# A fused transformer block: shared-expert products moved among the last expert tiles, gathers re-paced, eight scatters held

## The chip, the cores and the metric

One core of a Trainium2 chip runs the whole program. The metric is the device time of one execution in microseconds; lower is better.

## What is computed

The input x has 4 batches of 512 tokens of 256 values. The block is feed-forward, attention, feed-forward, each with a residual:

```python
x = x + 0.5 * ffn(layernorm(x))
x = x + attention(layernorm(x))          # 16 heads of 128, weights as codes times scales
x = x + 0.5 * ffn(layernorm(x))
# ffn(h):
probs = softmax(h @ router_w.T)                              # 16 experts
topk_w, topk_idx = top_k(probs, 2); topk_w /= sum(topk_w)
shared = (silu(h @ shared_gate_w) * (h @ shared_up_w)) @ shared_down_w     # width 256
routed = for each token, sum over its 2 experts e of
         topk_w * (silu(h @ gate_w[e]) * (h @ up_w[e])) @ down_w[e]        # width 128
ffn = shared + routed
```

## The kernel before, in words

Each engine has a program of its own, written out by hand in one order, and semaphores tie the programs together; nothing else sets the order. f = 0 is the first feed-forward, f = 1 the second. The change touches f = 1 alone.

Values are kept as a high and a low part, and a product is three passes of TensorE (`product`, L1703 to L1705): high by high, high by low, low by high. So each result is first copied by ScalarE (the high part) and then subtracted by VectorE (the low part).

**Routing.** Batch by batch, rows of X are normalized, transposed (L1714), copied by ScalarE (`xt_hi`, L850) and split by VectorE (`xt_lo`, L1171); TensorE makes the router's logits (L1729 to L1732), VectorE chooses two experts for each token (`choose`; its last step, `marked`, L1210, raises `hot1`), and ranks and counts give each token its place. GpSimd scatters the normalized rows to `xs_dram`, in order of experts: four scatters of 128 rows for each of two choices, eight to a batch (`to_experts`, L597; for the first two batches `place`, L738). One more transfer (L793) fills the space behind each expert's rows. Scatters of batches 0 to 2 raise `scat0`, those of batch 3 `scat_3`. In the meantime SP loads the expert weights, 16 transfers of 768 KB.

**Expert tiles.** A tile is 128 rows of one expert; 48 tiles are worked in 24 pairs. SP loads the tiles (`tile_loads`, L494): it waits for the table `toff1`, for all of `scat0`, and ahead of pair 4 for `scat_3` and the fill. For pair p, TensorE transposes the rows of pair p + 1 (L1809), makes the gate and up products of pair p, transposes h of pair p - 1 (L1834) and makes the down product of pair p - 2. ScalarE copies rows (L876), applies SiLU (L888), copies h (L893) and evicts the result (L899, raises `r_ev`); VectorE splits (L1358, L1382) and multiplies (L1370). SP stores each pair's result to `y_tiles` (L465).

**Shared expert.** A step is one batch, in two products k (`gate_up(f, k)`, step k // 2): 12 multiplications of 512 columns each: a gate bank and an up bank, and for each two row blocks of the input in three passes. ScalarE applies SiLU (`shared`, L863), VectorE multiplies (`shared_mul`, L1338), ScalarE copies and VectorE splits (`shared_hi`, L868; `shared_lo`, L1343), TensorE makes the down product of the step (`down`, 24 multiplications of 256 columns), and VectorE adds it to X (`shared_add`, L1350). Products 0 to 3 come ahead of the tiles, `down(1, 1)` behind the first pair, products 4 to 7 and two down products behind the last pair.

**Combining.** GpSimd gathers each token's two rows from `y_tiles` (`fetch`, L605), eight gathers to a batch, and VectorE adds each, times its weight, to X (`combine_block`, L1395). Batch 0 is combined beside pairs 21 to 23, the others behind the pairs. `stored` waits until the tiles that a batch needs are in `y_tiles`; the counts for that are loaded into registers from `need`. Gathers are paced by `r_ev`: those of batch 0 one to a pair from pair 9 on. SP writes each half batch of X out when it is done.

## Time and profile before

| | us |
|---|---|
| median of 3 runs (1068.46 to 1069.44) | 1068.58 |
| the profiled execution, its own time | 1071.48 |
| its span | 1069.7 |
| TensorE busy | 980.6 (92% of the span) |
| VectorE busy | 798.7 (75%) |
| ScalarE busy | 676.3 (63%) |
| GpSimd busy | 626.3 (59%) |

The granted clock of TensorE over the span is 0.964 of full speed. The page gives shares over the whole program; a change in one stage is read from the rows of that stage. In the order of time, a row has its start, its duration, engine, line and operation, what is written and read, and in brackets how long the engine was idle before it and what released it. "issue" means that the profile shows nothing that it waited for, "remote" that the release came from something that the profile doesn't pair with an instruction. A line can be that of a helper, so that L1703 to L1705 stand for all three-pass products.

### The profile page before, as it was taken

Reading aid. Unit: us, or ns where it says so; the run is one execution under the profiler, and the core shown is the slowest. Engines: PE = TensorE matmul, PEld = TensorE weight load, DVE = VectorE, ACT = ScalarE, POOL = GpSimd, SP = SyncE. Lnnn points to the kernel's source line nnn. Section 1 sums busy time; section 2 is a strip of 40 time slices with the busy share of each in tenths; the row PEclk is TensorE's granted clock in tenths of the full one; section 3 lists DMA queues with packets and bytes.
Section 4 is the critical chain, followed back from the end, with each engine's and each line's share of the span. In section 5 each row is a group of like instructions: output and inputs, shape, how many; then the busy total and the mean of one; then the engine's idle time right before and its main releaser. Section 6 shows DMA issues by size and latency. Waiting matters only on the chain. (4 is left out here: it accounts for less than half of the span.)

```text
span 1069.7 us, 18752 instructions
## 1 busy us (share of the span) xinstructions
PE 980.6 (92%) x5314; PEld 844.7 (79%) x5314; DVE 798.7 (75%) x1682; ACT 676.3 (63%) x1485; POOL 626.3 (59%) x916
## 2 busy tenths in 40 slices
PE   5669999899999999999999999999999997579995
PEld 4459987677888888888888888888888885469985
DVE  7777577788887777787777877778788876358545
ACT  5545645667776777777776777767777765135641
POOL 1740458776436876767787666787536377630252
PEclk9769999999999999999999999999999999879997
DMA  9877652766456675787768877777754469966653
GB/s 313 286 254 236 199 188 69 152 152 115 79 100 142 138 128 105 188 182 182 150 142 210 216 190 159 172 149 185 162 97 80 87 146 197 391 234 197 194 177 104
DMA packets 329891, 183.07 MB, mean 171 GB/s; under 512 B 273344, under 2 KB 314944, under 8 KB 329152
## 3 DMA queue, kind: packets, MB, share of 16 engines
q1 hardware_dynamic: 323056, 155.66, 59.8%
q0 software_dynamic: 6432, 20.98, 5.9%
q10 hardware_dynamic: 304, 5.24, 1.4%
q8 instruction: 46, 0.75, 0.3%
q14 instruction: 53, 0.43, 0.1%
HBM read 73.31 MB, written 46.92 MB: 112 GB/s over the span
## 5 line engine op out<-in xcount | busy, mean ns | idle before, releaser
L669 POOL CAST R<-turned 128x512 fp32r<-128x512 f16 x512 | 290.5, 617 | 215.2 <-DMA turned<-work 152.4
L1703 PE MATMUL bank<-R 128*128 128x512 f32 (+2 forms) x1056 | 391.7, 371 | 25.3 <-DVE R L1343 10.0
L1704 PE MATMUL bank<-R 128*128 128x512 f32 (+2 forms) x1056 | 380.7, 360 | 0.0
L1705 PE MATMUL bank<-R 128*128 128x512 f32 (+2 forms) x1056 | 379.7, 360 | 0.0
L1703 PEld LDWEIGHTS bank<-R 128*128 128x128 f32 x1056 | 206.0, 195 | 59.5 <-issue 13.8
L1705 PEld LDWEIGHTS bank<-R 128*128 128x128 f32 x1056 | 205.7, 195 | 28.3
L1704 PEld LDWEIGHTS bank<-R 128*128 128x128 f32 x1056 | 206.2, 195 | 26.7
L975 ACT ACTIVATE bank<-bank,soft 128x512 f32<-128x512 f32 x256 | 170.3, 667 | 70.6 <-DVE soft L1515 70.6
L1508 DVE SCALAR_TENSOR_TENSOR R<-bank,bias,R 128x512 fp32r<-128x512 f32 x192 | 143.7, 749 | 68.5 <-ACT R L995 37.5
L1515 DVE TENSOR_REDUCE soft<-bank 128x1 f32<-128x512 f32 x256 | 168.6, 686 | 25.1 <-PE bank L1705 25.1
L1529 DVE SCALAR_TENSOR_TENSOR work<-bank,soft,work 128x512 f16<-128x512 f32 x256 | 185.1, 742 | 0.8 <-ACT work L988 0.8
L988 ACT ACTIVATE work<-bank,soft 128x512 f16<-128x512 f32 x256 | 161.5, 683 | 14.4 <-DVE soft L1523 14.1
L605 POOL DMA_INDIRECT R<-y_tiles,gpos x48 | 46.5, 969 | 124.7 <-ACT work L899 66.3
L1940 PE MATMUL bank<-R 128*128 128x512 f32 x256 | 104.6, 409 | 9.0 <-POOL R L669 7.3
L1941 PE MATMUL bank<-R 128*128 128x512 f32 x256 | 102.3, 400 | 0.0
L1942 PE MATMUL bank<-R 128*128 128x512 f32 x256 | 101.5, 396 | 0.0
L995 ACT ACTIVATE R<-bank,bias 128x512 fp32r<-128x512 f32 x64 | 44.1, 689 | 82.0 <-PE bank L1942 82.0
L969 ACT ACTIVATE R<-bank,bias 128x512 fp32r<-128x512 f32 x128 | 87.1, 681 | 0.0
L597 POOL DMA_INDIRECT xs_dram<-work,pos x48 | 50.6, 1053 | 48.4 <-DVE pos L1219 34.6
L1957 PE MATMUL bank<-R 128*128 128x256 f32 x256 | 72.3, 282 | 3.4 <-DVE R L1508 3.4
L1959 PE MATMUL bank<-R 128*128 128x256 f32 x256 | 72.4, 283 | 0.0
L1958 PE MATMUL bank<-R 128*128 128x256 f32 x256 | 72.4, 283 | 0.0
(164 smaller groups left out, 1379.2 us busy)
## 6 DMA issues: line engine op xcount, KB each, us to landing
work<-in_parts SPq DMA_DIRECT2D x64, 256.0 KB, 4.1
work<-in_ffn_w SPq DMA_DIRECT2D x34, 384.0 KB, 4.8
work<-xs_dram SPq DMA_DIRECT2D x96, 128.0 KB
y_tiles<-work SPq DMA_DIRECT2D x48, 256.0 KB
w_dram<-work SPq DMA_DIRECT2D x16, 768.0 KB, 4.6
R<-w_dram SPq DMA_DIRECT2D x16, 768.0 KB
y_tiles<-in_empty ACTq DMA_DIRECT2D x2, 2176.0 KB
X<-in_x SPq DMA_DIRECT2D x4, 512.0 KB, 4.9
```

Source lines behind the costliest of these rows:

```text
L669: nc.gpsimd.tensor_copy(whole_into(m, l, kb), whole_block(m, u, l, kb)).then_inc(s["cast_pool"], 1)
L975: nc.scalar.activation(s_bank(m, qb)[:], s_bank(m, qb)[:], ACT.Exp, bias=m.mx[:, qb:qb + 1], scale=1.0, accum_out=m.sm[:, qb:qb + 1]).then ...
L988: nc.scalar.activation(m.planes[:, qb, 0, :], s_bank(m, qb)[:], ACT.Copy, scale=m.ri[:, qb:qb + 1])\
L1508: v_.scalar_tensor_tensor(out=dst[:, 1, :], in0=bank[bk][:], scalar=m.bias[:, which, h:h + 1], in1=dst[:, 0, :].bitcast(F32), op0=ALU.add, ...
L1515: v_.reduce_max(m.mx[:, qb:qb + 1], s_bank(m, qb)[:], AX_X, negate=True).then_inc(s["max"], 1)
L1529: v_.scalar_tensor_tensor(out=m.planes[:, qb, 1, :], in0=s_bank(m, qb)[:], scalar=m.ri[:, qb:qb + 1], in1=m.planes[:, qb, 0, :], op0=ALU.m ...
L1703: nc.tensor.matmul(out, ah, bh, start=(i == 0 and first), stop=False)
L1704: nc.tensor.matmul(out, ah, bl, start=False, stop=False)
L1705: last = nc.tensor.matmul(out, al, bh, start=False, stop=(i == n - 1))
L1940: nc.tensor.matmul(bank[1][:], vh, ph, start=(kb == 0), stop=False)
L1941: nc.tensor.matmul(bank[1][:], vh, pl, start=False, stop=False)
L1942: ins = nc.tensor.matmul(bank[1][:], vl, ph, start=False, stop=(kb == QB - 1))
```

## The change

Six things, all in f = 1.

1. Shared products 4 and 5 are made inside the pair loop: product 4 at the pair index 23, product 5 at 24, each ahead of a pair's down product; ScalarE's and VectorE's steps of them go along. Products 6 and 7 follow the loop, ahead of both down products.
2. Own buffers: products 4 to 7 have banks 2 and 3 as gate banks (in place of 4 and 5), step 3 takes banks 0 and 1 for up and 4 and 5 for its down product, and step 2's h goes to `hT2`. Step 3's down product no longer waits for step 2's sums; the copy of its h waits for the last pair's down product instead.
3. The sums of step 3 come ahead of the second half of batch 3's combining, not behind all of it.
4. Gathers: two to a pair for each batch, from pairs 9, 16 and 20; before, one to a pair for batch 0 from pair 9, and two to a pair from 17 and 21. Batch 3's gathers wait for its stores and for product 5 alone, not for one of the products 4 to 7 each. The twelve counts are loaded at once.
5. Batch 3's gathers land in the part of xT that holds the tokens of batch 2, not in the experts' weights.
6. The eight scatters of the third batch wait for `hot1` = 4, the choice of the fourth batch.

```diff
 def shared_banks(f, step):
+    if (f, step) == (1, 3):
+        return 0, 4
     return (6, 0) if f == 0 and step < EARLY[0] else (0, 6)
+
+def gate_bank(m, f, k):
+    late = f == 1 and k >= 2 * EARLY[1]
+    return m.bank[(2 if late else 4) + k % 2]

 def turned_h(m, f, step):
-    return m.hT2 if (f, step) == (1, 1) else m.hT
+    return m.hT2 if (f, step) in ((1, 1), (1, 2)) else m.hT

-LANDING = {(0, 0): 0, (0, 2): 2, (0, 3): 3, (1, 0): 0, (1, 1): 1}
+LANDING = {(0, 0): 0, (0, 2): 2, (0, 3): 3, (1, 0): 0, (1, 1): 1, (1, 3): 2}
...
@@ pool_program
     pool.wait_ge(s["pos1"], 1)
+    pool.wait_ge(s["hot1"], QB)
     to_experts(1, 2, 0)
     to_experts(1, 2, 1)
...
-    stored(1, 0)
-    pool.wait_ge(s["gu"], 2 * QB + 2)
-    for j in range(TOPK * QB):
-        pool.wait_ge(s["r_ev"], NPAIR + SLOW_FROM + j)
-        fetch(1, 0, j)
-    stored(1, 1)
+    pool.wait_ge(s["need"], 2)
+    _, counts = nc.values_load_multi_w_load_instructions(
+        m.need[0:1, 0:RESULTS * B], engines=[POOL_ENGINE], min_val=16, max_val=2 * PUT_F)
+
+    def gathers(b, first):
+        for sem, n in zip(m.put, counts[RESULTS * b:RESULTS * (b + 1)]):
+            pool.wait_ge(sem, n)
+            pool.sem_inc(s["there"], 1)
+        pool.wait_ge(s["gpos"], TOPK * B + TOPK * (b + 1))
+        for j in range(TOPK * QB):
+            if first is not None:
+                pool.wait_ge(s["r_ev"], NPAIR + first + j // 2)
+            fetch(1, b, j)
+
     pool.wait_ge(s["gu"], 2 * QB + 4)
-    for j in range(TOPK * QB):
-        pool.wait_ge(s["r_ev"], NPAIR + SLOW_FROM + 8 + j // 2)
-        fetch(1, 1, j)
-    stored(1, 2)
+    gathers(0, SLOW_FROM)
+    gathers(1, SLOW_FROM + 7)
     pool.wait_ge(s["r_xt"], NPAIR + MOST)
-    for j in range(TOPK * QB):
-        pool.wait_ge(s["r_ev"], NPAIR + SLOW_FROM + 12 + j // 2)
-        fetch(1, 2, j)
-    stored(1, 3)
-    pool.wait_ge(s["r_dn"], 2 * NPAIR)
-    for j in range(TOPK * QB):
-        pool.wait_ge(s["gu"], 3 * QB + 1 + j // 2)
-        fetch(1, 3, j)
+    gathers(2, SLOW_FROM + 11)
+    pool.wait_ge(s["gu"], 2 * QB + 6)
+    gathers(3, None)
@@ act_program, shared_hi
-        wait(act, s["dn"], 2 * QB * f + 2 * (k // 2))
+        if (f, k // 2) == (1, 3):
+            act.wait_ge(s["r_dn"], 2 * NPAIR)
+        else:
+            wait(act, s["dn"], 2 * QB * f + 2 * (k // 2))
@@ act_program, tiles, ahead of the eviction
+            if f == 1 and p == NPAIR - 1:
+                shared(1, 4)
+            if f == 1 and p == NPAIR:
+                shared_hi(1, 4)
+                shared(1, 5)
@@ act_program, behind tiles(1)
-    for k in range(2 * EARLY[1], 2 * QB):
-        shared(1, k)
-        shared_hi(1, k)
+    shared_hi(1, 5)
+    shared(1, 6)
+    shared(1, 7)
+    shared_hi(1, 6)
+    shared_hi(1, 7)
@@ dve_program, tiles, at the end of a pair
+            if f == 1 and p == NPAIR - 1:
+                shared_mul(1, 4)
+            if f == 1 and p == NPAIR:
+                shared_mul(1, 5)
+                shared_lo(1, 4)
@@ dve_program, behind tiles(1)
-    shared_h(1, 4)
+    shared_lo(1, 5)
     combine_half(1, 1, 0)
-    shared_h(1, 5)
     combine_half(1, 1, 1)
-    shared_h(1, 6)
+    shared_mul(1, 6)
+    shared_mul(1, 7)
     shared_add(1, 2)
+    shared_lo(1, 6)
+    shared_lo(1, 7)
     combine_half(1, 2, 0)
-    shared_h(1, 7)
     combine_half(1, 2, 1)
     combine_half(1, 3, 0)
-    combine_half(1, 3, 1)
-    dve.wait_ge(s["comb1"], 2 * B)
     st.settle()
     shared_add(1, 3)
+    combine_half(1, 3, 1)
@@ pe_program, down
-            wait(pe, s["x_add"], 2 * QB * f + 2 * (step - 1) + i + 1)
+            if (f, step) != (1, 3):
+                wait(pe, s["x_add"], 2 * QB * f + 2 * (step - 1) + i + 1)
@@ pe_program, tiles, ahead of the down product of pair p - 2
+            if f == 1 and p in (NPAIR - 1, NPAIR):
+                gate_up(1, 4 + p - NPAIR + 1)
@@ pe_program, behind tiles(1)
-    gate_up(1, 4)
-    gate_up(1, 5)
+    gate_up(1, 6)
+    gate_up(1, 7)
     pe.wait_ge(s["r_ev"], 2 * NPAIR)
-    gate_up(1, 6)
     down(1, 2)
-    gate_up(1, 7)
     down(1, 3)
```

**ScalarE, the last two pairs and what follows.** L867 of the change is L863 of before (SiLU of a shared product), L875 is L868 (the copy of h), L895, L900 and L911 are L888, L893 and L899 (SiLU, copy and eviction of a pair). Before:

```order
L888 ACTIVATE work<-bank 128x256
L893 ACTIVATE R<-bank 128x256
L899 ACTIVATE work<-bank 128x512
L893 ACTIVATE R<-bank 128x256
L899 ACTIVATE work<-bank 128x512 x2
L863 ACTIVATE work<-bank 128x512
L868 ACTIVATE R<-work 128x512
L863 ACTIVATE work<-bank 128x512
L868 ACTIVATE R<-work 128x512
```

and now:

```order
L895 ACTIVATE work<-bank 128x256
L900 ACTIVATE R<-bank 128x256
L867 ACTIVATE work<-bank 128x512
L911 ACTIVATE work<-bank 128x512
L900 ACTIVATE R<-bank 128x256
L875 ACTIVATE R<-work 128x512
L867 ACTIVATE work<-bank 128x512
L911 ACTIVATE work<-bank 128x512 x2
L875 ACTIVATE R<-work 128x512
L867 ACTIVATE work<-bank 128x512 x2
L875 ACTIVATE R<-work 128x512 x2
```

The SiLUs of products 4 and 5 stand ahead of the evictions of pairs 21 and 22; those of 6 and 7 follow each other.

**VectorE, the end of its program.** L1352 is L1338 of before (multiply), L1357 is L1343 (split), L1364 is L1350 (sums), L1416 is L1395 (combining; eight rows of it are a batch). Before:

```order
L1338 TENSOR_TENSOR work<-bank,work 128x512
L1343 TENSOR_TENSOR R<-work,R 128x512
L1395 SCALAR_TENSOR_TENSOR X<-R,wt,X 128x256 x4
L1338 TENSOR_TENSOR work<-bank,work 128x512
L1343 TENSOR_TENSOR R<-work,R 128x512
L1350 SCALAR_TENSOR_TENSOR X<-bank,X 128x512 x2
L1395 SCALAR_TENSOR_TENSOR X<-work,wt,X 128x256 x4
L1338 TENSOR_TENSOR work<-bank,work 128x512
L1343 TENSOR_TENSOR R<-work,R 128x512
L1395 SCALAR_TENSOR_TENSOR X<-work,wt,X 128x256 x4
L1395 SCALAR_TENSOR_TENSOR X<-R,wt,X 128x256 x8
L1350 SCALAR_TENSOR_TENSOR X<-bank,X 128x512 x2
```

and now:

```order
L1352 TENSOR_TENSOR work<-bank,work 128x512
L1396 TENSOR_TENSOR R<-bank,R 128x256
L1352 TENSOR_TENSOR work<-bank,work 128x512
L1357 TENSOR_TENSOR R<-work,R 128x512 x2
L1416 SCALAR_TENSOR_TENSOR X<-R,wt,X 128x256 x8
L1352 TENSOR_TENSOR work<-bank,work 128x512 x2
L1364 SCALAR_TENSOR_TENSOR X<-bank,X 128x512 x2
L1357 TENSOR_TENSOR R<-work,R 128x512 x2
L1416 SCALAR_TENSOR_TENSOR X<-work,wt,X 128x256 x8
L1416 SCALAR_TENSOR_TENSOR X<-R,wt,X 128x256 x4
L1364 SCALAR_TENSOR_TENSOR X<-bank,X 128x512 x2
L1416 SCALAR_TENSOR_TENSOR X<-R,wt,X 128x256 x4
```

The multiplications of products 4 and 5 have moved into the loop, both splits of a step stand together, and the last sums stand ahead of the last four blocks.

**GpSimd, from the second batch's scatters to the fill, with the semaphores that a row waits for.** L601 is L597 of before, L742 is L738, L798 is L793. Before:

```order
L738 DMA xs_dram<-work,pos 34944x256 x5
L597 DMA xs_dram<-work,pos 34944x256 [waits pos1]
L597 DMA xs_dram<-work,pos 34944x256 x7
L597 DMA xs_dram<-work,pos 34944x256 [waits xn_dve1,xn_act1,pos1]
L597 DMA xs_dram<-work,pos 34944x256 x7
L793 DMA xs_dram<-R,fill 8945664x1 [waits e_in,behind]
```

and now:

```order
L742 DMA xs_dram<-work,pos 34944x256 x5
L601 DMA xs_dram<-work,pos 34944x256 [waits hot1,pos1]
L601 DMA xs_dram<-work,pos 34944x256 x7
L601 DMA xs_dram<-work,pos 34944x256 [waits xn_dve1,xn_act1,pos1]
L601 DMA xs_dram<-work,pos 34944x256 x7
L798 DMA xs_dram<-R,fill 8945664x1 [waits e_in,behind]
```

No row moves; the first scatter of the third batch waits for `hot1` too, and everything behind it with it.

## Rows read from the trace of the kernel before

**Rows 1.** The profile's page of the kernel before, its head.
```profile
span 1069.7 us, 18752 instructions
```

**Rows 2.** Busy time by engine in three stretches; then granted clock, DMA share, GB/s.
```profile
1010.00:1020.00 10.00, 10.00 (x89) 10.00 (x87) 5.09 (x11) 6.51 (x16) 3.61 (x4) 1.00 0.47 144
1040.00:1050.00 10.00, 6.32 (x29) 5.08 (x28) 5.48 (x12) 2.51 (x5) 5.71 (x7) 0.87 0.51 159
936.00:938.00 2.00, 1.82 (x9) 1.83 (x9) 0.89 (x3) 1.99 (x3) 0.00 (x0) 0.50 1.02 425
```

**Rows 3.** TensorE in order of time, tail: start, us, what, [idle before <- releaser].
```profile
1030.44 0.38 PE L1834 MATMUL bank<-cst,work 128*128 128x128 f32 x2
1042.36 0.39 PE L1703 MATMUL bank<-R 128*128 128x512 f32 x1
1048.93 0.58 PE L1703 MATMUL bank<-R 128*128 128x256 f32 x1 [3.68 <-DVE R L1343]
1054.22 0.41 PE L1703 MATMUL bank<-R 128*128 128x512 f32 x1
```

**Rows 4.** ScalarE in order of time, tail.
```profile
1046.16 0.60 ACT L863 ACTIVATE work<-bank 128x512 f32<-128x512 f32 x1 [4.34 <-PE bank L1705]
1049.79 0.60 ACT L863 ACTIVATE work<-bank 128x512 f32<-128x512 f32 x1 [1.64 <-remote]
```

**Rows 5.** VectorE in order of time, its last work.
```profile
1062.31 3.45 DVE L1395 SCALAR_TENSOR_TENSOR X<-R,wt,X 128x256 f32<-128x256 f32 x8
1065.79 1.29 DVE L1350 SCALAR_TENSOR_TENSOR X<-bank,X 128x512 f32<-128x512 f32 x2
```

**Rows 6.** GpSimd's gathers in the tail (four of 32), and all 32 to landing.
```profile
1042.81 0.96 POOL L605 DMA_INDIRECT R<-y_tiles,gpos  x1 [0.30 <-issue]
1044.08 0.95 POOL L605 DMA_INDIRECT R<-y_tiles,gpos  x1 [0.30 <-issue]
1047.65 0.95 POOL L605 DMA_INDIRECT R<-y_tiles,gpos  x1 [0.31 <-issue]
1058.76 0.95 POOL L605 DMA_INDIRECT R<-y_tiles,gpos  x1 [0.30 <-issue]
...
DMA to landing us min/median/max: 2.8/2.8/3.6
```

**Rows 7.** GpSimd in the front: first and last of two unbroken series (13 and 9).
```profile
916.28 0.98 POOL L738 DMA_INDIRECT xs_dram<-work,pos  x1 [0.16 <-issue]
931.52 0.96 POOL L597 DMA_INDIRECT xs_dram<-work,pos  x1 [0.30 <-issue]
943.97 0.96 POOL L597 DMA_INDIRECT xs_dram<-work,pos  x1 [11.48 <-DVE pos L1219]
954.13 0.96 POOL L793 DMA_INDIRECT xs_dram<-R,fill  x1 [0.31 <-issue]
```

**Rows 8.** ScalarE and VectorE in order of time, front.
```profile
934.80 1.08 ACT L850 ACTIVATE R<-bank 128x512 fp32r<-128x512 f32 x2 [7.58 <-remote]
...
941.74 0.22 DVE L1210 TENSOR_TENSOR A<-hot 128x64 bf16<-128x64 f32 x1
...
956.90 0.60 ACT L876 ACTIVATE R<-bank 128x512 fp32r<-128x512 f32 x1 [3.11 <-remote]
```

**Rows 9.** TensorE in order of time, front.
```profile
927.28 1.09 PE L1714 MATMUL bank<-cst,work 128*128 128x128 f32 x8 [0.57 <-issue]
950.17 0.28 PE L1703 MATMUL bank<-R 128*128 128x256 f32 x1
953.04 0.60 PE L1809 MATMUL bank<-cst,work 128*128 128x128 f32 x4
```

**Rows 10.** SP's queue, the second layer's tile loads.
```profile
948.18 24.17 SPq L494 DMA_DIRECT2D work<-xs_dram  x24
```

**Rows 11.** The first expert layer: ScalarE's copy, and GpSimd's last scatter before it.
```profile
43.63 0.60 ACT L850 ACTIVATE R<-bank 128x512 fp32r<-128x512 f32 x1 [2.24 <-remote]
...
40.91 1.23 POOL L597 DMA_INDIRECT xs_dram<-work,pos  x1 [0.30 <-issue]
```

More of the change, by code:

```diff
@@ L226, in build @@
         m.yb = Yw[:, 0:TOPK * QB * D].rearrange("p (b k t d) -> p b k t d", b=1, k=TOPK, t=QB)
-        m.yx = R[:, O_Z:O_Z + TOPK * QB * D].bitcast(F32).rearrange("p (k t d) -> p k t d", k=TOPK, t=QB)
         m.xna = Yw[:, TOPK * QB * D:2 * TOPK * QB * D].rearrange("p (b t d) -> p b t d", b=2, t=QB)
@@ L341, in landing @@
         return m.xT[:, k, i // 2, at:at + D].bitcast(F32)
-    if (f, b) == (1, B - 1):
-        return m.yx[:, k, i, :]
     return m.yb[:, 0, k, i, :]
@@ L862, in shared @@
         wait(act, s["h_lo"], 2 * QB * f + k - 1)
-        nc.scalar.activation(shared_place(m, f, k), halves(bank[4 + k % 2][:]), ACT.Silu).then_inc(s["silu"], 1)
+        nc.scalar.activation(shared_place(m, f, k), halves(gate_bank(m, f, k)[:]), ACT.Silu).then_inc(s["silu"], 1)
     def shared_hi(f, k):
         act.wait_ge(s["h"], 2 * QB * f + k + 1)
-        wait(act, s["dn"], 2 * QB * f + 2 * (k // 2))
+        if (f, k // 2) == (1, 3):
+            act.wait_ge(s["r_dn"], 2 * NPAIR)
+        else:
+            wait(act, s["dn"], 2 * QB * f + 2 * (k // 2))
         nc.scalar.activation(halves(turned_h(m, f, k // 2)[:, k % 2, 0, :]), shared_place(m, f, k), ACT.Copy).then_inc(s["h_hi"], 1)
@@ L1392, in combine_block @@
                 dve.wait_ge(s["x_add"], 2 * QB * f + 2 * (b + 1))
+            if (f, b, k) == (1, B - 1, 1):
+                dve.wait_ge(s["x_add"], 4 * QB)
             st.settle()
@@ L1768, in gate_up @@
         tok = slice(step * S, (step + 1) * S)
-        for g, out in ((0, bank[4 + j]), (1, bank[shared_banks(f, step)[0] + j])):
+        for g, out in ((0, gate_bank(m, f, k)), (1, bank[shared_banks(f, step)[0] + j])):
             last = product(nc, out[:], [(Wg[0][:, kt, g, j * P:(j + 1) * P], Wg[1][:, kt, g, j * P:(j + 1) * P],
```

## Prediction

> **What bounds the kernel now.** I read, in this order, the page's head, the busy time in stretches, and the instructions in order of time of the second expert layer, engine by engine: first its tail, then its front. The profiled execution has a span of 1069.7 us [rows 1] and took 1071.48 us; the median of the runs shown is 1068.58, so 2.9 is taken off at the end.
>
> The change touches only what comes after 920 us. In the middle of the pair loop TensorE is busy without a gap, and nothing there can be won [rows 2]. Behind the loop it is different: between 1040 and 1050 TensorE is busy for 6.32 of 10 us and VectorE for 5.48 [rows 2]. Everybody waits in turn. Products 4 and 5 stand behind the loop; product 6 ends at 1045.2 and TensorE then stands for 3.68 us until VectorE has split product 5 (L1343); it runs the down product of step 2 until 1054.2, then product 7 [rows 3]. The split of product 5 was late because the SiLU of product 5 (ACT L863) started only at 1046.16, though the matrix multiplications of product 5 end at 1042.36 and ACT had nothing else to do; that of product 6 starts at 1049.79, 4.5 us behind its product [rows 4]. VectorE's last work, eight blocks of combining and two sums, runs from 1062.31 to 1067.08 [rows 5]. GpSimd issues a gather each 1.25 us; the eight of the last batch are issued from 1042.81 on, each pair behind one of the products 4 to 7, so that the last goes out at 1058.76 and lands 2.8 us later [rows 6].
>
> In the front the chain is: normalized rows, transposes (TensorE, 927.28 to 928.4) [rows 9], copy (ACT L850, at 934.80, after 7.58 us of idle), logits, choice (DVE L1210, 941.74) [rows 8], the tables, the tile loads (SP, from 948.18) [rows 10], the first transposes of rows at 953.04 [rows 9], their copy (ACT L876) at 956.90 [rows 8], and behind it the first expert product.
>
> **One reading decides much of it.** ACT starts 6.4 us after the transposes of 927.28 have ended, and 3.3 us after those of 953.04, with "remote" as the releaser, i.e. nothing that the profile pairs. Both times GpSimd is in an unbroken series of indirect transfers: 916.28 to 932.48 and 943.97 to 955.09 [rows 7]; both times the wait ends 1.8 to 2.3 us behind the series. The first expert layer has it too: a copy at 43.63 after 2.24 us of such a wait, the series over at 42.14 [rows 11]. The two late SiLUs of the tail also lie in such a series [rows 4, 6]. I read this as: TensorE's signals reach others late while GpSimd issues for long. Signals early in a series come in time, so the series has to have run for some us. It is an inference from coincidences.
>
> **The change, part by part.**
>
> *Products 4 and 5 among the last pairs; step 3's banks.* Count from 1030.82, when TensorE has the transposes of pair 22 done [rows 3]. A product is 12 multiplications of 512 columns. Number 6 starts at 1042.36 and is over at 1048.93 - 3.68 = 1045.25, 2.89 us; its last multiplication counts there with its whole 0.39, though the next starts 0.23 after it, so a product takes 2.73. A pair's down product is 6 of 256 columns; a step's is 24, which took 2.87 us at 2.4 GHz (950.17 to 953.04, [rows 9]) and 5.3 us at 1.2 GHz (1048.93 to 1054.22, [rows 3]); six are thus 0.72. In the new order: product 4 to 1033.5, down and transposes to 1034.5, product 5 to 1037.2, two down products to 1038.7, product 6 to 1041.4, product 7 to 1044.1, down of step 2 to 1047.0. Before, these ended at 1057.0 (product 7) and 1054.2. No work is added; the same work goes into TensorE's gaps. The loop itself pays: the evictions of the last two pairs (ACT L899) stand behind a SiLU that waits for product 4, and one behind product 5: the last comes at 1039.4, not 1037.5. Banks 2, 3, 0, 1 are free then, hT2 too, and the wait for the sums that step 3's down product had is gone; all that costs nothing.
>
> VectorE then has the chain: SiLU 7 (0.6) to 1044.8, multiply (0.69) to 1045.5, two sums (1.29) whose second waits for the down product, to 1047.7, two splits (0.69 each, overlapping) to 1049.0, then combining at 3.45 / 8 = 0.43 a block [rows 5]: batch 2 to 1052.4, the first half of batch 3 to 1054.1, step 3's sums to 1055.4 (its down product runs 1049.0 to 1051.9, or 1054.3 at 1.2 GHz: hidden under the combining), the second half of batch 3 to 1057.1. Against 1067.08 that is **-10.0**. The output transfer behind it is as before.
>
> *Gathers.* Batch 0 now goes two to a pair instead of one; batches 1 and 2 start one pair earlier. Batches 1 and 2 are read behind the loop, so this wins nothing by itself. Batch 3 waits for its stores alone: last eviction 1039.4, then the store. Its landing isn't shown; between nothing and the longest landing of a gather, 3.6 [rows 6]; I take 3, since a store is such a transfer. Eight gathers from 1042.4, at 1.25, and 2.8 to land: the last at 1054.0, just ahead of its use at 1055.4. Hidden, with 1.4 us to spare. Reading all twelve counts at once costs twelve register loads in time when GpSimd has nothing to do.
>
> *Late signals in the tail.* The series from 1042.4 to 1052.4 covers the signals of product 7 (1044.1) and of the step-2 down product (1045.5 and 1047.0). Bounds: nothing (early signals in a series are prompt), and until the series ends (a sum at 1053.6 in place of 1047.7 puts the end at 1064.5). I take one late signal of the size between the two ends that product 5 showed, 1042.36 to 1046.16, less the usual 0.1: 3.7; on the chain it costs 2.7, since VectorE was going to wait about 1.0 for the down product anyway. Tail: -10.0 + 2.7 = **-7.3**.
>
> *The third batch's scatters held until the fourth choice.* Eight scatters of 1.27 leave 922.6 to 932.5 and stand behind hot1 = 4. If my reading holds, the copy at 934.80 comes at 928.5: 6.3 earlier. The logits behind it run at 1.2 GHz now, after the long gap [rows 2]; at 2.4 they would save 1 us or so, an estimate. The choice then falls at about 934.5 instead of 942. But now 16 scatters and the fill are one series, 934.5 to 956.1 (17 x 1.27), and the loads must wait for the first eight: 934.5 + 10.2, and 2 to 3 to land, 947, about what SP shows now (948.18). TensorE has its down product of step 0 done by 946 (7 earlier), gets rows at about 950, and its signal for the copy falls deep into the series: late until 956.1 and the 1.1 to 2.3 that the rows show behind a series, 957.6, against 956.90 now. Held scatters and earlier choice cancel: between -6.5 (that signal comes in time) and +8.4 (rival 3). I take **+0.7**, because it is nearest to the rows of both series.
>
> Sum: 1069.7 - 7.3 + 0.7 = 1063.1 of span; 1064.9 for that execution; **1062.0** for the median.
>
> **Rivals.**
> 1. *The hold wins twice* (0.15): the early choice and no late signal at the first copy. For it: signals 6 us into a series are still prompt. Against: this one would be 15 us in. 1062.0 - 0.7 - 6.5 = 1054.8.
> 2. *The last batch binds* (0.15): signals in the tail stay late until its eight gathers are out. For it: 1046.16 and 1049.79 are both 1.1 to 1.2 behind the end of a gather that ended a series [rows 4, 6] (gathers until 1045.03 and 1048.60). Then 2.6 of the tail's gain remains: 1068.58 - 2.6 + 0.7 = 1066.7.
> 3. *Slower: the scatters are put in front of the first tile* (0.25). If the copy at 934.80 is late for another reason, the choice stays at 941.96. Then the first eight scatters run 942.1 to 952.3 and land at 954: the loads start 6 later, and the series ends at 963.7. The first copy comes between 961 and 965.3 instead of 956.90: +4 to +8.4. With the tail's -7.3 to -2.6 that is 1065.3 to 1074.4, around 1069.5. It decides the sign from about 955 on: if the loads start later than that, little is left of the tail's gain. For it: those transfers share the memory system with the expert loads, and the copy's lateness may be theirs; against: the copy came at 934.80, while the DMA engines were full until 938 at least [rows 2].
> That the change does nothing is excluded by its own order of instructions.
>
> A rule of the Trainium skill speaks for the third rival: "SBUF — State Buffer", Who interferes with whom, says that only VectorE and GpSimd share ports and that "PE and ACT never wait on anyone". By that rule a scatter can't be what keeps ACT from copying TensorE's result, and the hold only delays: the time of rival 3. The rows side against it: five waits of ACT that end with a series [rows 4, 8, 11]; but they show when, not why, which is why the rival keeps a quarter.
>
> **How the numbers follow.** Forecast 0.45, rivals 0.15, 0.15, 0.25. A measurement of this kernel can tell 0.2% (2.1 us) from no change. Forecast and rivals 1 and 2 are faster by more than that: 0.75. Rival 3 I split over its range: slower 0.18, within 0.2% 0.07. The range leaves out the far ends of rivals 1 and 3: 1053.5 to 1071. The forecast's own range is 1059.3 (no late signal in the tail) to 1065.
>
> **What would show it.** Right: ACT L850's copy of the fourth batch within 1 us of its transposes, the choice at 934 to 936; SP's loads from 946 to 948; TensorE without a gap over 1 us from 1031 to 1047; gathers of batch 3 from 1042 in one series; last sums at 1055, last combining at 1057 to 1060. Wrong: the copy still at 934 or later and SP's loads at 953 or later (rival 3); the first copy of rows at 951 (rival 1); VectorE's sums of step 2 at 1053 or later (rival 2); evictions in the loop delayed by batch 0's denser gathers, which I cost at nothing because one gather a pair costs TensorE nothing there now [rows 2]; each late signal could open a gap.

## The result, and the profile after

| | before | changed |
|---|---|---|
| median of 19 runs each, us | 1068.46 | 1072.84 |
| ratio, 95% interval | | 1.0050 (1.0037 to 1.0063) |
| profiled execution, us | 1071.48 | 1075.79 |
| its span, us | 1069.7 | 1074.0 |

The change is slower by 0.5%; the forecast was 1062.0 and faster, and 1072.84 lies above the whole range given (1053.5 to 1071). Three points in the program cut both traces into stages: the transposes of the fourth batch (TensorE, [rows 9]), the first expert product, the transposes of pair 22 ([rows 3], first row), and VectorE's last end ([rows 5]).

| us | before | changed | difference |
|---|---|---|---|
| transposes of the fourth batch | 927.28 | 925.09 | -2.2 |
| from there to the first expert product | 31.66 | 33.45 | +1.8 |
| from there to the transposes of pair 22 | 71.50 | 81.37 | +9.9 |
| from there to VectorE's end | 36.64 | 31.58 | -5.1 |

The changed code has nothing ahead of the first point, so its -2.2 is the scatter between executions. The loss is in the pair loop, which the prediction had costed at nothing.

ScalarE of the changed kernel in order of time (L854, L883 and L895 are L850, L876 and L888 of before: the copy of the fourth batch, the first copy of expert rows, the SiLU of a pair):

```profile
925.78 1.08 ACT L854 ACTIVATE R<-bank 128x512 fp32r<-128x512 f32 x2 [0.75 <-PE bank L1735]
...
956.53 0.60 ACT L883 ACTIVATE R<-bank 128x512 fp32r<-128x512 f32 x1 [10.84 <-PE bank L1831]
...
1006.71 0.38 ACT L895 ACTIVATE work<-bank 128x256 f32<-128x256 f32 x1 [4.48 <-remote]
...
1030.96 0.38 ACT L895 ACTIVATE work<-bank 128x256 f32<-128x256 f32 x1 [5.62 <-remote]
```

The copy now follows its transposes after 0.75 us of idle instead of 7.58 [rows 8]; the copy of expert rows is late instead; and two SiLUs of the loop come 4.5 and 5.6 us late. GpSimd (first and last of four unbroken series: 17 transfers, 6, 6 and 10 gathers):

```profile
932.34 0.96 POOL L601 DMA_INDIRECT xs_dram<-work,pos  x1 [12.68 <-DVE A L1224]
...
952.77 0.96 POOL L798 DMA_INDIRECT xs_dram<-R,fill  x1 [0.30 <-issue]
...
998.03 0.99 POOL L609 DMA_INDIRECT R<-y_tiles,gpos  x1 [44.31 <-ACT work L911]
...
1004.35 0.95 POOL L609 DMA_INDIRECT R<-y_tiles,gpos  x1 [0.30 <-issue]
...
1022.41 0.94 POOL L609 DMA_INDIRECT R<-y_tiles,gpos  x1 [12.10 <-ACT work L911]
...
1028.66 0.95 POOL L609 DMA_INDIRECT R<-y_tiles,gpos  x1 [0.30 <-issue]
...
1048.35 1.16 POOL L609 DMA_INDIRECT work<-y_tiles,gpos  x1 [1.51 <-ACT work L911]
...
1059.99 0.95 POOL L609 DMA_INDIRECT R<-y_tiles,gpos  x1 [0.30 <-issue]
```

Both late SiLUs start 1.4 us behind the end of a series of six. Two gathers take 2.5 us and a pair 2.8 us, so that "two to a pair" is an unbroken series. Both end after six because of the lateness itself: the seventh gather waits for an eviction that stands behind the late SiLU in ScalarE's program (L911 at 1007.25 and 1031.50). TensorE's busy time in stretches (the columns of [rows 2]), and its rows in time:

```profile
1007.60:1010.40 2.80, 2.80 (x13) 2.68 (x14) 1.63 (x4) 1.90 (x5) 1.89 (x2) 0.50 0.52 157
1010.00:1020.00 10.00, 10.00 (x85) 10.00 (x84) 4.57 (x10) 6.13 (x14) 0.31 (x1) 0.96 0.40 129
1026.00:1031.00 5.00, 2.87 (x25) 2.67 (x23) 0.06 (x1) 0.04 (x1) 2.84 (x3) 1.00 0.51 152
1032.00:1037.00 5.00, 5.00 (x24) 4.88 (x25) 3.36 (x8) 2.34 (x6) 3.28 (x4) 0.50 0.53 160
1040.00:1050.00 10.00, 10.00 (x56) 8.66 (x55) 4.61 (x11) 4.96 (x10) 4.67 (x6) 1.00 0.45 140
```
```profile
1007.60 0.69 PE L1856 MATMUL bank<-cst,work 128*128 128x128 f32 x2 [2.02 <-DVE work L1384]
...
1031.85 0.47 PE L1856 MATMUL bank<-cst,work 128*128 128x128 f32 x1 [2.98 <-DVE work L1384]
...
1039.91 0.38 PE L1856 MATMUL bank<-cst,work 128*128 128x128 f32 x2
...
1063.15 0.58 PE L1724 MATMUL bank<-R 128*128 128x256 f32 x1 [6.64 <-DVE R L1357]
```

A late SiLU costs more than its own wait: TensorE stands for 2.98 us and then works at a granted clock of 0.50 (1.2 GHz) from 1032 to 1037. The first late SiLU does the same: a gap of 2.02 us and a clock of 0.50 from 1007.60 to 1010.40. Gaps of 5.0 us and about 9 us of work at half clock, half of which is lost (my estimate from these rows), are near the loop's 9.9. In the tail TensorE has no gap (10.00 of 10 us from 1040 to 1050, against 6.32 before) until its last product. VectorE's tail:

```profile
1061.20 0.69 DVE L1364 SCALAR_TENSOR_TENSOR X<-bank,X 128x512 f32<-128x512 f32 x1 [4.25 <-remote]
...
1069.82 1.67 DVE L1416 SCALAR_TENSOR_TENSOR X<-R,wt,X 128x256 f32<-128x256 f32 x4 [0.45 <-DVE X L1364]
```

The second sum of step 2 waits for a product that TensorE ended at 1056.5, until the last gather is out (1060.94). One thing has to be known to read the numbers below: executions of this kernel came in two kinds. With late signals of TensorE, as in both profiles here, the kernel before takes 1067 to 1072 us; without any, 1044 us. Kernels measured together fell on one kind, and each is compared with runs of the kernel before beside it.

### The profile page after: what moved, and what is told of

It reads as the page before. It is cut to its first block, busy times and chain, and to the rows that moved or that the text cites. A ratio compares the mean times of both kernels' runs of the same rounds, so it can differ in the third digit from the quotient of the medians.

```text
span 1074.0 us, 18747 instructions
## 1 busy us (share of the span) xinstructions
PE 981.6 (91%) x5314; PEld 845.6 (79%) x5314; DVE 798.2 (74%) x1682; ACT 675.4 (63%) x1485; POOL 624.8 (58%) x916
## 3 DMA queue, kind: packets, MB, share of 16 engines
q0 software_dynamic: 6432, 20.98, 6.1%
## 4 chain that ended last, share of the span: by engine, by line
PE 59%; issue 8%; DVE 7%; ACT 6%; DMA 2%; POOL 2%; another core or an unknown queue 1%; SPq 1%; DVEq 0%; ACTq 0%; POOLq 0%
PE bank L1724 13%; PE bank L1726 13%; PE bank L1725 12%; PE bank L1964 5%; PE bank L1965 4%; PE bank L1966 4%; ACT bank L987 3%; PE bank L1983 2%; PE bank L1981 2%; PE bank L1982 2%; DMA turned<-work 2%; POOL R L673 1%; DVE work L1550 1%; DVE X L1416 1%
## 5 line engine op out<-in xcount | busy, mean ns | idle before, releaser
L601 POOL DMA_INDIRECT xs_dram<-work,pos x48 | 50.6, 1054 | 49.7 <-DVE pos L1233 23.3
L1981 PE MATMUL bank<-R 128*128 128x256 f32 x256 | 72.8, 285 | 3.4 <-DVE R L1529 3.4
```

## The experiments

Theory A: a long unbroken series of GpSimd's indirect transfers makes TensorE's signals late, and the new pace of gathers makes such series in the loop. Its rivals stand with each run.

### The parts one by one

In `pace_before` the gathers have their old paces; `tail_alone` also drops the hold; `hold_alone` and `pace_alone` are the kernel before with one part.

```diff
 pace_before (from the change)
-                pool.wait_ge(s["r_ev"], NPAIR + first + j // 2)
+                pool.wait_ge(s["r_ev"], NPAIR + first + (j if b == 0 else j // 2))
-    gathers(1, SLOW_FROM + 7)
+    gathers(1, SLOW_FROM + 8)
-    gathers(2, SLOW_FROM + 11)
+    gathers(2, SLOW_FROM + 12)
 tail_alone, further
-    pool.wait_ge(s["hot1"], QB)
 hold_alone (from before)
+    pool.wait_ge(s["hot1"], QB)
 pace_alone (from before)
-        pool.wait_ge(s["r_ev"], NPAIR + SLOW_FROM + j)
+        pool.wait_ge(s["r_ev"], NPAIR + SLOW_FROM + j // 2)
...
-        pool.wait_ge(s["r_ev"], NPAIR + SLOW_FROM + 8 + j // 2)
+        pool.wait_ge(s["r_ev"], NPAIR + SLOW_FROM + 7 + j // 2)
...
-        pool.wait_ge(s["r_ev"], NPAIR + SLOW_FROM + 12 + j // 2)
+        pool.wait_ge(s["r_ev"], NPAIR + SLOW_FROM + 11 + j // 2)
```

> The change with the paces of before: batch 0's gathers one to a pair from pair 9, batch 1's two to a pair from 17, batch 2's from 21. In the changed kernel's trace the stretch from the first expert product to the transposes of pair 22 takes 81.4 us (958.54 to 1039.91) against 71.5 before, with SiLUs of the pairs late by 4.48 and 5.62 us beside two series of six gathers. Theory A (the pace makes the series, the series make TensorE's signals late): that stretch is 71.5 to 73 again, no SiLU ahead of 1015 waits over 1.5 us, and the time is 1068.5 + 2.0 (front) - 5.1 (tail) = 1065.4, ratio to before 0.996 to 0.998. Rival B (the late signals come from something else in the change, such as the hold or the banks, and the gathers only coincide): the stretch stays at 79 to 82 and the ratio at 1.003 to 1.007.

> As pace_before, and the third batch's scatters not held: of the change only the late products, their buffers and the order of the tail are left. If the hold costs the 2.0 us that the two traces give for the front (first expert product 0.4 us earlier on a trace that is 2.4 us ahead at 920), this one is 1063.4, ratio 0.994 to 0.996, about 2 us below pace_before. If the hold costs nothing, both are the same within 1 us. If the tail's gain is smaller than the 5.1 us of the trace, both move up together.

> The kernel before with the one wait added: the third batch's scatters stand behind the fourth choice. Theory A: the copy of the fourth batch comes within 1 us of its transposes (6 us earlier), the choice 8 us earlier, but the first copy of expert rows waits until 2 to 3 us behind the last scatter; first expert product 1 to 3 us later, time 1069.5 to 1071.5, ratio 1.000 to 1.003. Rival: the early choice is a gain that the rest of the change took back; then 1060 to 1066, ratio below 0.998.

> The kernel before with the change's paces for batches 0, 1 and 2 alone (two to a pair from pairs 9, 16, 20); batch 3's gathers, the products and the scatters as before. Theory A: series of five or six gathers near 998 and 1018, each with a SiLU of a pair late by 4 to 6 us; the stretch of the pairs 7 to 10 us longer, time 1075 to 1079, ratio 1.006 to 1.010. Rival B: 1067 to 1070, ratio 0.999 to 1.001.

| | ratio to before | loop, us | tail, us |
|---|---|---|---|
| pace_before | 0.9963 (0.9945 to 0.9980) | 72.81 | 32.43 |
| tail_alone | 0.9973 (0.9954 to 0.9993) | 71.68 | 30.14 |
| hold_alone | 1.0033 (1.0017 to 1.0050) | 72.43 | 35.08 |
| pace_alone | 1.0035 (1.0016 to 1.0054) | 81.07 | 31.80 |

Loop and tail are the last two stages of the table above. With the old paces the loop is back, and so is the sign: 1.0050 / 0.9963 makes the new pace worth +0.9% in the change. Alone it costs 0.35%: its loop is as long as the change's, with the same two SiLUs late, but its tail is 4.8 us shorter than before's, since the gathers are further on. In the change the late products seem to have taken that gain already, so that only the cost is left: its tail is 31.58, and 32.43 with the old paces. I had expected 1.006 to 1.010 for it, and missed that. ScalarE of `pace_alone`:

```profile
1004.41 0.38 ACT L888 ACTIVATE work<-bank 128x256 f32<-128x256 f32 x1 [4.50 <-remote]
...
1029.08 0.38 ACT L888 ACTIVATE work<-bank 128x256 f32<-128x256 f32 x1 [5.68 <-remote]
```

`hold_alone` is slower by 0.33%: the hold is a loss by itself, and its early choice wins nothing. In its trace the front takes 33.07 us instead of 31.66, with the first copy of rows behind 10.82 us of idle. The other traces with late signals agree: the front takes 33.1 to 34.0 us in the seven with the hold (`front_gaps` left out) and 30.8 to 32.9 in the six without it. Without the hold, `tail_alone` isn't measurably better than `pace_before`; that figure of mine (2 us) stays unconfirmed there.

### Series or gathers, issuing or data

```diff
 twos (from the change; in threes the same with j % 3)
+            if b < 2 and j > 0 and j % 2 == 0:
+                pool.wait_ge((m.y_first, m.y_in)[(j - 1) // QB][b], 16 * (QB + (j - 1) % QB + 1))
             fetch(1, b, j)
 short_rows (from the change)
+        cols = slice(0, 32) if f == 1 and b < 2 else slice(0, D)
-            out=landing(m, f, b, k, i), out_offset=None, in_=m.y_tiles,
+            out=landing(m, f, b, k, i)[:, cols], out_offset=None,
+            in_=m.y_tiles.rearrange("n (a c) -> (n a) c", c=32) if f == 1 and b < 2 else m.y_tiles,
```

> The change with the same paces, but in batches 0 and 1 every second gather waits until the ones before it in its batch have landed: no series is longer than two, and the gathers are as many. Theory A: the SiLUs that came 4.48 and 5.62 us late in the change come within 1 us (at most 1.5) everywhere ahead of pair 21, TensorE has no gap over 1 us from 972 to 1022, and the stretch from the first expert product to the transposes of pair 22 takes 72 to 75 us instead of 81.4. Rival D (the lateness comes with the gathers of batches 0 and 1 as such, of any spacing): two SiLUs are still late by 3 us or more.

> The change with the gathers of batches 0 and 1 cut to 32 of 256 values a row (so batches 0 and 1 of the output leave most of the routed part out): an eighth of the bytes in the same number of instructions and descriptors. Theory A1 (it is GpSimd's issuing that holds TensorE's signals up): the series of six are there as before, and SiLUs of the pairs are late by 4.5 and 5.6 us again, stretch 80 to 82 us. Theory A2 (it is the data that the gathers move, reading y_tiles and writing to SBUF): both waits shrink below 2 us and the stretch is 72 to 75 us.

`twos`: from 965 us on no SiLU of a pair waits over 1.2 us; the loop takes 70.35 us, 11 less than the change's, though GpSimd issues 14 gathers in it (19 in the change's loop, two series of six among them). Gathers as such don't make a SiLU late, and rival D is out. The other 18 of the 32 form one series behind the loop. GpSimd (first and last of it), ScalarE's SiLU of product 7, VectorE's sums of step 2, TensorE's last product:

```profile
1035.94 0.95 POOL L609 DMA_INDIRECT R<-y_tiles,gpos  x1 [4.48 <-ACT work L913]
...
1057.35 0.95 POOL L609 DMA_INDIRECT R<-y_tiles,gpos  x1 [0.30 <-issue]
...
1051.76 0.60 ACT L869 ACTIVATE work<-bank 128x512 f32<-128x512 f32 x1 [9.10 <-remote]
...
1061.69 1.29 DVE L1366 SCALAR_TENSOR_TENSOR X<-bank,X 128x512 f32<-128x512 f32 x2 [8.61 <-remote]
...
1064.23 0.58 PE L1726 MATMUL bank<-R 128*128 128x256 f32 x1 [16.62 <-DVE R L1359]
```

TensorE had ended the product behind that sum at 1047.6, 14 us before; VectorE was free for it from 1053.1 on. So the lateness moved with the series: out of the loop, into the tail, and the time was 1076.83 (one run). It also corrects my reading: the SiLU at 1051.76 got its signal in the middle of the series. "Late until the series is over" is too simple.

`short_rows` (its batches 0 and 1 leave out most of the routed part) moves an eighth of the bytes with the same six gathers in a row. Beside the first series the wait is in two parts, ahead of a copy of rows and ahead of the SiLU, 4.7 us together; beside the second the SiLU is late as before:

```profile
1010.14 0.60 ACT L884 ACTIVATE R<-bank 128x512 fp32r<-128x512 f32 x1 [2.27 <-PE bank L1832]
...
1013.16 0.38 ACT L896 ACTIVATE work<-bank 128x256 f32<-128x256 f32 x1 [2.42 <-remote]
...
1037.34 0.38 ACT L896 ACTIVATE work<-bank 128x256 f32<-128x256 f32 x1 [5.76 <-remote]
```

The loop takes 80.89 us, as in the change. So it isn't the bytes that are moved. GpSimd's issuing and the packets of its queue, nearly as many as before (6176 against 6432 over the whole program), are not told apart by this run; where I write "issuing" below, it is the two together.

### Two repairs

`front_gaps` and `tail_order` start from `pace_before`.

```diff
 front_gaps
     to_experts(1, 3, 0)
-    to_experts(1, 3, 1)
+    pool.wait_ge(s["r_xhi"], NPAIR + 1)
+    place(3, 1, 0)
+    place(3, 1, 1)
+    pool.wait_ge(s["r_xhi"], NPAIR + 2)
+    place(3, 1, 2)
+    place(3, 1, 3)
 tail_order, combine_block
-            if k == 0 and (f, b) != (1, B - 1):
+            if k == 0 and (f, b) not in ((1, B - 1), (1, 2)):
                 dve.wait_ge(s["x_add"], 2 * QB * f + 2 * (b + 1))
+            if (f, b, k) == (1, 2, 1):
+                dve.wait_ge(s["x_add"], 2 * QB + 6)
 tail_order, dve_program
-    shared_add(1, 2)
     shared_lo(1, 6)
     shared_lo(1, 7)
     combine_half(1, 2, 0)
+    st.settle()
+    shared_add(1, 2)
```

> pace_before with two pauses in the held scatters: the fourth batch's first four follow the third's eight at once, the next two wait for ScalarE's copy of the first pair's rows, the last two and the fill for that of the second pair. In pace_before the rows are transposed at 946.62, the copy comes at 954.43, the first expert product at 956.44. Theory A (TensorE's signals are held up by an unbroken series of GpSimd's transfers, and by nothing else): the copy comes within 1 us of the transposes, the first product at 950 to 951.5; the last scatters go out 5 us later (956 instead of 951) and may hold up pair 4's loads by 0 to 3 us. Time 1058 to 1061, 3 to 5.5 us below pace_before, ratio 0.990 to 0.994. Rival C (the copy waits for the transfers themselves, such as the loads of rows and scatters in flight, and not for GpSimd's issuing): the copy stays at 952 or later, and the later scatters make it a loss of 1 to 5 us, ratio 0.998 to 1.001.

> pace_before with another order of VectorE's tail: both splits of step 3 and the first half of batch 2's combining come ahead of step 2's sums. In pace_before the second of these sums waits until 1051.40 (4.31 us idle) for a product that TensorE ended at 1045.8, and TensorE then stands 7.53 us for the splits behind it. Theory A: the late signal stays (second sum still at 1050 to 1052), but VectorE has 3.0 us of work ahead of it and TensorE's last product is over by 1049; what is left behind the sum is 3 halves of combining and two sums, 6.3 us, so the end comes 3 to 4 us earlier: ratio 0.992 to 0.994. Rival: the last gathers land at 1055 and another late signal (step 3's product) takes the place: under 1.5 us, ratio 0.995 to 0.997.

`front_gaps` 0.9975 (0.9947 to 1.0003), `tail_order` 0.9971 (0.9944 to 0.9999): neither shows the gain that I expected. In `front_gaps` the rows are transposed from 947.03 on and copied at 948.16 (first row), as theory A has it and not as rival C, and the transposes of pair 22 come 3.5 us earlier than in `pace_before` (measured from the first point); the tail gives it back (VectorE's second sum, TensorE's last product):

```profile
948.16 0.60 ACT L888 ACTIVATE R<-bank 128x512 fp32r<-128x512 f32 x1 [2.56 <-PE bank L1836]
...
1051.50 0.69 DVE L1369 SCALAR_TENSOR_TENSOR X<-bank,X 128x512 f32<-128x512 f32 x1 [7.10 <-issue]
...
1053.45 0.58 PE L1729 MATMUL bank<-R 128*128 128x256 f32 x1 [10.65 <-DVE R L1362]
```

Its tail is 35.6 us long against 32.43 in `pace_before`: the same late sum. In `tail_order` TensorE no longer waits behind that sum, and the tail is 31.14.

### The other kind of execution

```diff
 both_orders = front_gaps and tail_order together
 pause_in_tail (from both_orders)
+            if (b, j) == (B - 1, 4):
+                pool.wait_ge(s["x_add"], 2 * QB + 6)
             fetch(1, b, j)
 both_twos = both_orders with the wait of twos
```

> front_gaps and tail_order together. In front_gaps the loop was over 3.5 us earlier than in pace_before, and the tail gave it back: the second sum of step 2 came at 1051.50, after 7.10 us of idle, behind a series of twelve gathers that ended at 1049.88, and TensorE's last product waited 10.65 us for the splits behind that sum. Theory A: with the splits and half a batch of combining ahead of the sums, only two sums and three halves of combining (6.3 us) stand behind the late signal: VectorE ends at 1057 to 1059 on front_gaps' clock of events (1061.8 there), 3 to 4 us below front_gaps, ratio 0.991 to 0.994. Rival: each part's gain lies in the same place and only one of the two counts: ratio 0.996 to 0.998, as each alone.

> both_orders with a pause of GpSimd in batch 3's gathers: the last four wait for VectorE's two sums of step 2. Theory A: the series ends some 5 us earlier and lets TensorE's signal through 1 to 1.5 us behind its end or at once, if the product ends later; the second sum comes 3 us or more earlier than in both_orders, but the last gather goes out 2 us later (and lands 2.8 us behind that), so that the end moves by -2 to +1 us. What counts here is the sum's time against the end of the shortened series. Rival E (the lateness has its own length, whatever the series does): the second sum comes no earlier than in both_orders, and the end is 2 us or more later.

> both_orders with batches 0 and 1 in series of two at most (every second gather waits until those before it in its batch have landed), at the paces of the kernel before. Theory A: the SiLUs that are late in the loop of both_orders (2.8 us near 998, 3.1 us near 1020, 2.3 us near 1025) all come within 1.5 us; the loop is 1 to 3 us shorter. Batch 1's last gather goes out 1 to 4 us later, and the gathers behind it, so that the tail may give back as much: ratio 0.986 to 0.993. Rival: the late SiLUs in the loop come at other places instead, and the loop is as long as in both_orders.

> As twos, with series of three: the change with batches 0 and 1 in series of three at most. Series of two left no SiLU late, series of four one of 3.1 to 3.3 us, series of six one of 4.5 to 5.7. Theory A: a series of three is 3.5 us long, and a SiLU falls late by at most 2.8 (the 2.83 us behind three gathers in front_gaps), at one or two places of the loop; stretch of the pairs 71 to 74 us. If the lateness comes only where more gathers follow within a few us, none is late by over 1.5.

All four fell on executions in which the kernel before took 1043.95: ratios 1.0108, 1.0111 and 1.0144, and 1057.29 us for `threes`. None of ScalarE, VectorE and TensorE waits for a "remote" release for over 1.3 us from 890 us on, in series of up to 18. What they were meant to tell of late signals stays open (the dose of `threes`, the pause). But they show another bound: in `both_orders` VectorE's last combining waits 2.55 us for gathers to land, in `both_twos` the last two wait 4.24 and 1.40.

> The kernel before, unchanged, for a second profile of it. The last four kernels (both_orders, pause_in_tail, both_twos, threes) ran on another chip, on which the kernel before took 1043.95 us (9 runs) instead of 1067 to 1072, and no trace of the four had a copy or SiLU waiting for a 'remote' release, in series of up to 17. Theory F (TensorE's late signals beside GpSimd's series are a property of the chip or its state): where this run takes about 1044, its trace has ScalarE's copy of the fourth batch within 1 us of the transposes (6.4 us late on record), the choice 6 us earlier, no SiLU of a pair or of a shared product over 1 us late; where it takes 1066 to 1072, all of these are late as on record. A run of about 1044 with the late copy in it, or one of 1068 without, would be against F.

> The change, unchanged, beside it. By theory F on a chip without late signals the hold has nothing to gain (the copy comes in time anyway) and puts eight scatters behind the choice: tile loads 6 to 8 us later; the tail still gains (10 us by the sum of the prediction, bounded by batch 3's gathers); the gathers' pace costs nothing. Together -4 to +4 us, unless the loads' delay costs more: both_orders, with the hold, took 12 us more than the kernel before there, so I expect 1052 to 1058, ratio 1.008 to 1.013. On a chip with late signals: ratio 1.003 to 1.007 as measured, with SiLUs late by 4.5 and 5.6 us.

`before_again` took 1043.99, `after_again` 1052.88, ratio 1.0070 (1.0050 to 1.0089; the 17 runs of the kernel before beside them took 1044.67), the profiles' spans 1041.0 and 1050.7. They ran on the chip that had given `pace_before` and its group 1067.59 for the kernel before: the kind isn't a property of the chip. The kernel before (transposes of the fourth batch, their copy, tile loads, first transposes of rows, first expert product, sums at the end):

```profile
920.19 1.09 PE L1714 MATMUL bank<-cst,work 128*128 128x128 f32 x8 [0.37 <-ACT work L841]
...
920.89 1.09 ACT L850 ACTIVATE R<-bank 128x512 fp32r<-128x512 f32 x2 [0.75 <-PE bank L1714]
...
933.93 15.94 SPq L494 DMA_DIRECT2D work<-xs_dram  x12
...
938.85 0.63 PE L1809 MATMUL bank<-cst,work 128*128 128x128 f32 x4
...
941.20 0.38 PE L1703 MATMUL bank<-R 128*128 x1 [0.72 <-issue]
...
1037.12 1.29 DVE L1350 SCALAR_TENSOR_TENSOR X<-bank,X 128x512 f32<-128x512 f32 x2
```

The changed kernel, the same kind:

```profile
921.51 1.09 PE L1735 MATMUL bank<-cst,work 128*128 128x128 f32 x8 [0.36 <-ACT work L845]
...
940.85 5.49 SPq L498 DMA_DIRECT2D work<-xs_dram  x8
...
944.13 1.08 PE L1831 MATMUL bank<-cst,work 128*128 128x128 f32 x4 [4.74 <-DMA work<-xs_dram]
...
961.17 1.08 PE L1831 MATMUL bank<-cst,work 128*128 128x128 f32 x4 [1.87 <-DMA work<-xs_dram]
...
1046.16 1.67 DVE L1416 SCALAR_TENSOR_TENSOR X<-R,wt,X 128x256 f32<-128x256 f32 x4 [0.45 <-issue]
```

Here the copy is prompt with the scatters ahead of it, so that the hold has nothing to win. It puts the loads 19.34 us behind the transposes instead of 13.74, and the first product 25.40 instead of 21.01. The loop takes 74.01 us against 68.69: TensorE comes out of a gap of 4.74 us, its mean granted clock is 0.74 from 946 to 952 and 0.76 from 952 to 966 where it is 1.00 in `before_again`, and it waits for rows again at 961.17. The tail is 26.91 us against 28.52. Sum, with 1.3 at the first point: 9.4 in the two traces, 8.2 in the medians. So there the front costs and what follows from it in the loop, not the pace: `both_orders`, `pause_in_tail` and `both_twos`, with the hold and the paces of before, have the same front (25.5 to 25.8 us) and loop (74.2 to 74.7 us), and no SiLU late. The tail is 1.6 shorter, in one trace of each kernel. That it is the hold rests on these traces; without late signals it wasn't run alone.

### The last group

> hold_alone a second time, for the kind of execution in which no signal of TensorE is late (the kernel before at about 1044 us). There before_again had its tile loads 13.74 us behind the transposes of the fourth batch and after_again 19.34 us; the transposes of pair 22 came 9.7 us later, measured from there, and after_again took 8.2 us more. Theory G (without late signals the hold alone makes the change slower, because the choice comes in time anyway and the first eight scatters now stand behind it): this takes 7 to 10 us more than the kernel before, ratio 1.007 to 1.010. Rival: the hold costs the 5.6 us of the loads or less, ratio up to 1.005. If this falls on executions with late signals (1066 to 1072): 1.002 to 1.005 as in hold_alone.

> pace_alone a second time. Theory G: without late signals two gathers to a pair cost TensorE nothing, as I had put it in the prediction: stretch of the pairs as in before_again, and the gathers that go out earlier help the tail at most a little; -2 to +0.5 us, ratio 0.998 to 1.0005. If with late signals: 1.002 to 1.006 as in pace_alone.

> tail_alone a second time: the late products without hold and pace. Without late signals the tail from the transposes of pair 22 to VectorE's end takes 28.5 us in before_again and 26.9 in after_again. Theory G: -1 to -3 us, ratio 0.997 to 0.999. If the tail is bound by the gathers (32 of 1.25 us from 979 on), no gain: 0.999 to 1.001. If with late signals: 0.995 to 0.999 as in tail_alone.

> tail_alone with VectorE's order of tail_order (both splits and half a batch of combining ahead of step 2's sums), so without hold and with the paces of before: the version that the runs so far point to for both kinds of execution. With late signals: second sum and TensorE's last product no longer in one chain, 0.992 to 0.996. Without: no signal is late, so that the order wins what VectorE waits for the down product, under 1 us: 0.996 to 0.999, within 0.1% of tail_again.

The first three are `hold_alone`, `pace_alone` and `tail_alone` a second time; `tail_and_order` is `tail_alone` with VectorE's order of `tail_order`. All had late signals (before 1071.55), so that what they were to tell of the other kind stays open. `hold_again` 1.0019 (1.0006 to 1.0033), `pace_again` 1.0018 (1.0001 to 1.0035), `tail_again` 0.9950 (0.9932 to 0.9968), `tail_and_order` 0.9908 (0.9891 to 0.9926), 1062.69 us: the best of those with late signals, and faster than both kernels. The loops once more part by the pace: 80.9 to 81.9 us in the four traces with the new one and no pause (the change, `pace_alone`, `pace_again`, `short_rows`), 71.5 to 72.8 in eight with the old one. Only `front_gaps`, with late signals and the old pace, has 74.71. `tail_again`, VectorE and TensorE:

```profile
1055.91 0.69 DVE L1363 SCALAR_TENSOR_TENSOR X<-bank,X 128x512 f32<-128x512 f32 x1 [6.41 <-remote]
...
1057.85 0.58 PE L1723 MATMUL bank<-R 128*128 128x256 f32 x1 [11.39 <-DVE R L1356]
```

`tail_and_order`, the same sum, and VectorE's last work:

```profile
1053.27 0.69 DVE L1363 SCALAR_TENSOR_TENSOR X<-bank,X 128x512 f32<-128x512 f32 x1 [5.16 <-remote]
...
1058.74 1.67 DVE L1417 SCALAR_TENSOR_TENSOR X<-R,wt,X 128x256 f32<-128x256 f32 x4
```

The signal is still late; but the splits are made ahead of it, TensorE ends its last product at 1049.2 without a gap, and half a batch is combined. The tail is 31.10 us against 36.38. That tail difference is of two traces, and `tail_alone`, the same kernel as `tail_again`, had 30.14. By the medians the order wins 0.4% here, and not in `tail_order`, where the hold stood ahead of it; whether the hold is why wasn't tested. What hold, pace and this version are worth one by one without late signals wasn't measured.

## Why the prediction was wrong

**The reading of late signals** was right for this kind of execution, and became the cause of the result. The copy within 1 us of its transposes, the loads at 947 (945.06, on a trace 2.2 ahead), the first copy of rows deep in a series and late (forecast 957.6, measured 956.53, or 1.1 later from the first point): all as forecast. The front term, +0.7, measured +1.8 in the trace and 2.0 to 3.5 us by the ratios of `hold_again` and `hold_alone`.

**"One gather a pair costs TensorE nothing there now" is the step that failed.** It is true, [rows 2] show it, and it was used for two gathers a pair. By the numbers in hand, 2 x 1.25 = 2.5 us of 2.8, that is a series without an end. The term was put at 0 and measured +9.9 in the loop. The last paragraph of the prediction named the way ("each late signal could open a gap") and gave it neither a price nor a chance. The trace of before had the case in it, and I had not drawn on it: the first and last of four gathers in a row, and the SiLU behind them:

```profile
1017.97 0.94 POOL L605 DMA_INDIRECT R<-y_tiles,gpos  x1 [2.37 <-ACT work L899]
...
1021.73 0.95 POOL L605 DMA_INDIRECT R<-y_tiles,gpos  x1 [0.31 <-issue]
...
1023.74 0.38 ACT L888 ACTIVATE work<-bank 128x256 f32<-128x256 f32 x1 [3.26 <-remote]
```

**The tail.** TensorE's new order took from the transposes of pair 22 to the end of step 2's down product 16.2 us, as worked out (1030.82 to 1047.0). The late signal was put at 2.7 and cost 4.7 (1061.20 against 1056.5): -7.3 became -5.1. With the late products and late signals this tail is 30.1 to 36.4 us long (`tail_alone` and `tail_again`, the same kernel), so that one trace doesn't size this term. That was rival 2's mechanism. Two of the prediction's own numbers for it don't come out: a sum moved from 1047.7 to 1053.6 moves the end from 1057.1 to 1063.0, not to 1064.5; and rival 2 at 1066.7 was only 1.9 us below 1068.58, less than the 2.1 that a measurement was said to tell.

**Rival 3** had the sign, 1069.5, and the wrong place: the choice did come early. By the Trainium skill, "SBUF — State Buffer", Who interferes with whom, ScalarE and TensorE never wait on another engine for a port; `twos` and `pace_before` show that what they wait for can be late beside GpSimd's long series, which that rule doesn't speak of. In executions without late signals the rival's cost came out: the copy needs no help, the loads start 5.6 us later and the first product 4.4.

## What to carry to other kernels

Where a trace shows late signals of TensorE ("remote" waits of ScalarE or VectorE behind a product that has ended), multiply before re-pacing GpSimd's transfers: their number in a period by the time of one issue; close to the period it is an unbroken series, and what waits for TensorE inside it has to be priced, with the clock that TensorE loses in the gap. Put work that doesn't need the late signal ahead of the wait, and TensorE's next work off it (`tail_and_order`). And take a part's worth in the company it will have: the pace alone gave half its cost back in a tail that the other part had already shortened.

## What was not expected of the hardware

- TensorE's signals reached ScalarE and VectorE late beside series of GpSimd's indirect transfers: copies and SiLUs up to 7 or 8 us behind the end of what they waited for (a copy 7.3 in `hold_alone` and 7.8 in `short_rows`, a SiLU 7.0 in `twos`), a sum 9.4 us (`tail_again`) and one 14 us (`twos`). None was late in `twos`' series of two in the loop; SiLUs waited 2.8 us with three (`front_gaps`), 3.1 to 3.3 with four, mostly 4.5 to 5.8 with six. How long a break has to be isn't known: in the kernel before a SiLU came 4.5 us behind its product [rows 4] between a series of ten and one of two, 1.4 us apart. With an eighth of the bytes the wait was 5.76. Whether the signal is late or the product's last write isn't told apart; by the Trainium skill, "Perfetto Trace Analysis", Tensor Engine Instruction, the end in a profile is an estimate, and the update leaves only when PSUM has acknowledged the writes. No trace here shows that acknowledgement; they show that the end in the profile and the release lay 4.7 us apart in the changed kernel's tail and 14 in `twos`.
- The same kernel took 1068 us with this and 1044 without, on the same chip at different times, with the same two series in the front (13 and 9 transfers) and longer ones behind (8 and 14 gathers, where the slower trace has two of 4 and one of 10). From the first point the traces differ by 21.6 us: 10.7 in the front, 2.8 in the loop, 8.1 in the tail; 7.1 come before. So a long series is not enough by itself, and what sets the kind stays open.
